# Channel weights folded into the transposes of the products, values by key straight from the projection, and a larger share of channel 14 for VectorE

## The chip, the cores and the metric

The kernel runs on one core of a Trainium2 chip. The metric is the device time of one execution in microseconds (us), lower is better. The core has TensorE (PE; its weight loads are listed as PEld), VectorE (DVE), ScalarE (ACT), GpSimd (POOL) and a queue of DMA issues (SP). Each engine runs its own instructions in the order in which they are written, and they wait for one another by semaphores.

## The reference, cut to what matters

Batch 8, sequence 512, width 128, 16 heads of 8 dimensions, 16 channels. Everything is float32.

```
Q, K, V = proj(Wq, bq), proj(Wk, bk), proj(Wv, bv)       # per head
for wl in 16 channels:
    m = cos(phase_modulators)[wl, head]
    scores = einsum('bhqd,bhkd->bhqk', Q*m, K*m) * SCALE  # = m*m * (Q.K) * SCALE
    scores = scores * cos(KERR * scores * scores)
    attn = softmax(scores)
    acc += einsum('bhqk,bhkd->bhqd', attn, V) * interference_weights[wl]
combined = (acc / 16) @ Wo + bo
```

After that come a residual sum, normalisation, a shared feed-forward block and 8 gated experts on 256 of the rows. The cosine factor is 1 in float32 for small scores; the kernel bounds the scores on the chip and takes a fast way (the one that runs here) in which it is left out.

## The kernel before

**Units.** The work is cut into 32 units: a unit is one head for four of the eight batch rows. Units 0 to 15 are group 0, units 16 to 31 group 1. For one unit the scores of keys against queries, 128 partitions x 8192 columns (4 key tiles x 4 batch rows x 512 queries), stand in `s_t`. They are the same for all 16 channels up to the factor m*m, so each channel is one exponential over them with another scale.

**ScalarE** takes the exponentials of channels 0 to 13 of a unit over all 8192 columns (L656), and of channel 14 over the first 7168 (`ACT_LAST`, L653). It writes one of two buffers `probs`, so exponential w+2 waits until TensorE has used that of w (`pv_done`).

**TensorE** multiplies each channel's exponentials with the values of the unit (L1273): per channel 16 products of a 27-column stationary operand with 512 moving columns, each of them two instructions, so 32 instructions. The stationary operand is `v_pad`: for each of 32 tiles of 128 keys, nine columns (8 value dimensions and a one for the denominators) in a field of zeros, so that three channels share a bank of PSUM (six banks' worth per unit, `W_GROUPS`; the fifth holds channels 12 to 14 and the sixth channel 15).

**VectorE** takes what is left of the exponentials in pieces of seven operations each (`piece_dve`, L720 to L743): four pieces of 2048 columns for channel 15, and a fifth piece of 1024 columns, the rest of channel 14. TensorE multiplies the pieces (`piece_pe`, L756). VectorE also copies each of the six groups of products to SBUF (`copy_products`, L1413), TensorE transposes it (`turn_products`, L1243, four transposes), and VectorE divides by the denominators, multiplies with the channel's weight and sums up (`weigh`, L1422 to L1443: reciprocal, times weight, times products, sum).

**Preparation of the next unit** is spread over the steps w = 0 to 14 of a unit (`prep_pe`, `prep_dve`): step 1 projects q, k and v (L785, three times four products of 32 stationary columns with 512 moving ones, the four in different columns of the array) and adds the biases (L859 to L861); steps 2 to 5 take scores and their maxima; step 6 transposes v (L808) and the maxima (L815) and copies v into `v_pad` (L869); steps 8 to 11 take the scores again and copy them to `s_t` (L877).

**The order** is written by hand. In step w TensorE does: the product of a piece that is due (`PRODUCT_STEPS`), the products of channel w, the transposes that are due (`TURN_STEPS`), the preparation. VectorE does in step w: the operations of pieces that are due (`PIECE_STEPS`), a copy (`COPY_STEPS`), a division (`TURN_STEPS`), the preparation. Some are due after the unit's end, in steps 0 to 2 of the next: the transposes of copy 4 (which is channel 15 and is made after the last piece in step 14) in step 0, and the product of the fifth piece in step 1, before the products of channel 1. In group 1 a pair of units also carries one chunk of the feed-forward block (`FF_STEPS`): TensorE, VectorE and GpSimd take turns in it.

## Time and profile before

| | |
|---|---|
| three runs | 3448.43, 3453.41, 3458.12 us (median 3453.41) |
| profiled execution | 3451.96 us, span 3449.9 us |
| ACT busy | 3334.6 us, 97% |
| DVE busy | 3152.2 us, 91% |
| PE busy / PEld busy | 2711.8 us, 79% / 778.2 us, 23% |
| mean granted TensorE clock | 0.909 of full speed |

Busy shares are of the span. PE's busy time holds modelled ends of matmuls. Adjacent instructions of an engine overlap a little at their ends, so the distance between two starts is somewhat less than the duration. The granted clock of TensorE has two levels here, 1.00 (2.4 GHz) and 0.50 (1.2 GHz).

### The profile page before, as it was taken

What the parts mean: (1) busy time and instruction counts of PE and PEld (TensorE: products, weight loads), DVE (VectorE), ACT (ScalarE), POOL (GpSimd) and SP (SyncE); (2) the same over time, 40 slices, a digit from 0 to 9 for tenths busy, and PEclk for the clock granted to TensorE, in tenths of its full rate; (3) what the DMA queues carried; (4) which work ended last, traced back from release to release, by engine and by line L of the source; (5) the groups of instructions that cost most, each with busy time, mean ns of one, the idle gap of its engine ahead of it and who ended that gap; (6) DMA issues with size and microseconds to landing.
All of it is one profiled execution on the core that took longest, in us unless ns stands there. A gap on an engine that the chain in (4) does not pass through costs nothing.

```text
span 3449.9 us, 47792 instructions
## 1 busy us (share of the span) xinstructions
PE 2711.8 (79%) x20599; PEld 778.2 (23%) x20599; DVE 3152.2 (91%) x2977; ACT 3334.6 (97%) x610; POOL 199.5 (6%) x325
## 2 busy tenths in 40 slices
PE   7887778887778887778887788887888887888763
PEld 2222222222222222222222222222222222222222
DVE  8899899899899899899899999999999999999977
ACT  7999999999999999999999999999999999999971
POOL 0000000000000000000010011110011110011111
PEclk8899999999999999999999999999999899999886
DMA  1000000000000000000000000000000000000010
GB/s 50 1 1 1 1 1 1 1 1 1 1 1 1 1 1 1 1 14 1 1 3 1 4 2 4 2 4 1 2 4 2 4 2 1 4 2 4 2 30 28
DMA packets 20759, 16.10 MB, mean 5 GB/s; under 512 B 4225, under 2 KB 18962, under 8 KB 20306
## 3 DMA queue, kind: packets, MB, share of 16 engines
q1 hardware_dynamic: 19282, 12.34, 1.2%
q8 instruction: 165, 2.70, 0.3%
q10 hardware_dynamic: 1152, 0.53, 0.1%
q0 software_dynamic: 128, 0.26, 0.0%
q14 instruction: 32, 0.26, 0.0%
HBM read 7.76 MB, written 5.37 MB: 4 GB/s over the span
## 4 chain that ended last, share of the span: by engine, by line
ACT 61%; issue 30%; ACTq 4%; DVE 3%; PE 2%; DMA 0%; SPq 0%; POOL 0%; DVEq 0%; POOLq 0%
ACT probs L656 56%; ACT probs L653 4%; ACTq L646 4%; PE psum L1273 1%; DVE m_pad L865 0%; ACTq L650 0%; DVE s_t L877 0%; ACT probs L680 0%; DVE probs L1190 0%; DVE probs L928 0%; DMA iw<-nterference_weights_dram 0%; SPq L468 0%; DVE x_p L743 0%; DVE x_p L735 0%; DVE x_p L739 0%
## 5 line engine op out<-in xcount | busy, mean ns | idle before, releaser
L656 ACT ACTIVATE probs<-s_t 128x8192 f32<-128x8192 f32 x447 | 3101.2, 7090 | 2.2 <-PE psum L1273 2.2
L1273 PE MATMUL psum<-probs,v_pad 128*27 128x512 f32 x15232 | 1992.5, 665 | 602.5 <-ACT probs L656 583.8
L1273 PEld LDWEIGHTS psum<-probs,v_pad 128*27 128x27 f32 x15232 | 485.3, 115 | 2036.1 <-issue 1095.5
L723 DVE SCALAR_TENSOR_TENSOR x_y<-s_t,c_last,x_2k 128x2048 f32<-128x2048 f32 (+1 forms) x160 | 344.1, 2150 | 2.3
L735 DVE SCALAR_TENSOR_TENSOR x_p<-x_p,x_y 128x2048 f32<-128x2048 f32 (+1 forms) x160 | 332.6, 2079 | 4.5
L743 DVE SCALAR_TENSOR_TENSOR x_p<-x_p,x_2k 128x2048 f32<-128x2048 f32 (+1 forms) x160 | 332.1, 2075 | 3.9
L731 DVE SCALAR_TENSOR_TENSOR x_p<-x_y 128x2048 f32<-128x2048 f32 (+1 forms) x160 | 330.9, 2068 | 3.3 <-PE psum L756 3.3
L739 DVE SCALAR_TENSOR_TENSOR x_p<-x_p 128x2048 f32<-128x2048 f32 (+1 forms) x160 | 331.5, 2072 | 2.4
L877 DVE COPY s_t<-psum 128x2048 f32<-128x2048 f32 x128 | 292.2, 2284 | 21.8 <-PE psum L839 21.1
L865 DVE TENSOR_REDUCE m_pad<-psum 128x4 f32<-128x2048 f32 x128 | 292.4, 2286 | 10.8 <-PE psum L802 9.7
L756 PE MATMUL psum<-x_p,v_pad 128*27 128x512 f32 x1152 | 174.5, 620 | 51.9 <-DVE x_p L743 51.4
L653 ACT ACTIVATE probs<-s_t,ln_one 128x7168 f32<-128x7168 f32 x32 | 202.5, 6327 | 0.0
L720 DVE TENSOR_SCALAR x_2k<-s_t,c_last 128x2048 int16<-128x2048 f32 (+1 forms) x160 | 188.2, 1176 | 4.4 <-issue 1.0
L1422 DVE RECIPROCAL r_z<-psum 128x48 f32<-128x48 f32 (+1 forms) x192 | 80.2, 418 | 108.5 <-PE psum L1243 108.4
L1413 DVE COPY o_sb<-psum 128x512 f32<-128x512 f32 x192 | 131.4, 684 | 28.4 <-PE psum L1273 27.1
L802 PE MATMUL psum<-k_t,q_t 8*128 8x512 f32 x1024 | 147.7, 647 | 2.7 <-DVE m_pad L865 2.4
L839 PE MATMUL psum<-q_t,k_t 9*128 9x512 f32 x1024 | 147.6, 647 | 1.6 <-DVE s_t L877 1.5
L1243 PE MATMUL psum<-ident,o_sb 128*128 128x128 f32 x768 | 125.9, 286 | 1.0 <-DVE weighted L1429 1.0
L494 POOL COPY w_head<-w_qkv 128x24 f32 x32 | 27.7, 866 | 1659.6 <-ACT probs L656 1639.8
L1243 PEld LDWEIGHTS psum<-ident,o_sb 128*128 128x128 f32 x768 | 80.5, 141 | 166.0 <-issue 164.8
L727 DVE TENSOR_SCALAR x_2k<-x_2k 128x2048 int16<-128x2048 int16 (+1 forms) x160 | 105.0, 656 | 5.5
L505 POOL TENSOR_TENSOR loop_memory<-loop_memory 128x2 f32<-128x2 f32 x24 | 27.0, 1123 | 1415.8 <-DVE loop_memory L928 1415.8
(240 smaller groups left out, 1116.0 us busy)
## 6 DMA issues: line engine op xcount, KB each, us to landing
s_t<-in_L_attn_x_dram SPq DMA_DIRECT2D x4, 256.0 KB, 6.9
x_next_dram<-x_p SPq DMA_DIRECT2D x1, 1024.0 KB, 4.5
x_group<-x_next_dram SPq DMA_DIRECT2D x1, 1024.0 KB, 4.9
loop_memory<-in_L_attn_x_dram SPq DMA_DIRECT2D x8, 128.0 KB, 2.2
x_dram<-loop_memory SPq DMA_DIRECT2D x8, 128.0 KB, 1.8
out_dram<-loop_memory SPq DMA_DIRECT2D x8, 128.0 KB, 1.8
x_dram<-probs SPq DMA_DIRECT2D x2, 512.0 KB, 3.3
out_dram<-probs SPq DMA_DIRECT2D x2, 512.0 KB, 3.6
```

The costliest lines, as they stand in the source:

```text
L653: nc.scalar.activation(probs[:, (p + w) % 2, 0:ACT_LAST], s_t[:, p, 0:ACT_LAST], ACT.Exp, bias=ln_one[:, 0:1], scale=scales[(p + w) % 2]). ...
L656: nc.scalar.activation(probs[:, (p + w) % 2, :], s_t[:, p, :], ACT.Exp, scale=scales[(p + w) % 2]).then_inc(s["exp_done"], 1)
L720: nc.vector.tensor_scalar(at, scores, scale, LOWEST_Y, ALU.mult, ALU.max).then_inc(s["piece_chain"], 1)
L723: nc.vector.scalar_tensor_tensor(out=y, in0=scores, scalar=scale, in1=at, op0=ALU.mult, op1=ALU.subtract) \
L731: nc.vector.scalar_tensor_tensor(out=t, in0=y, scalar=EXP2_A, in1=y, op0=ALU.add, op1=ALU.mult) \
L735: nc.vector.scalar_tensor_tensor(out=t, in0=t, scalar=EXP2_B, in1=y, op0=ALU.add, op1=ALU.mult) \
L739: nc.vector.scalar_tensor_tensor(out=t, in0=t, scalar=EXP2_C, in1=t, op0=ALU.add, op1=ALU.mult) \
L743: nc.vector.scalar_tensor_tensor(out=t, in0=t, scalar=EXP2_D, in1=x_2k[:, 0:cols], op0=ALU.add, op1=ALU.mult) \
L865: nc.vector.tensor_reduce(m_pad[:, qt, :].rearrange("p (b l) -> p b l", l=L)[:, :, R_M:R_M + 1], banks(qt), AX.X, ALU.max, negate=True).th ...
L877: nc.vector.tensor_copy(s_t[:, p, kt * NB * S:(kt + 1) * NB * S], banks(kt).rearrange("p b q -> p (b q)")).then_inc(s["st_copied"], 1)
L1243: last = nc.tensor.transpose(psum[:, 6, qt * P:(qt + 1) * P], o_sb[:, at % 2, qt * P:(qt + 1) * P], ident[:])
L1273: last = nc.tensor.matmul(products_of(u, wg)[L * b:L * b + SLOTS * A, :], v_pad[:, p, b * T + kt, c0:c0 + SLOTS * A], probs[:, (p + w) % 2 ...
```

## The change

Three things are changed. (1) The products are no longer transposed against the identity and weighted afterwards: `turn_products` is now a matmul with a diagonal matrix (`turn_w`, one per group of channels, made once by `turn_weights_dve` in some 14 short operations before the first unit). Its diagonal has the channel's weight on the value rows and 1 on the denominators' rows, and the extra multiplication in `weigh` goes. (2) The values come by key straight from TensorE: 16 matmuls with 128 columns of `x_group` stationary and nine moving columns of the head's weights replace the third projection, the transposes of v and the copy into `v_pad`; the bias is added on the way into `v_pad`. (3) `SHARED_B` becomes (0, 1): VectorE's fifth piece has 2048 columns in group 0 and 1536 in group 1 instead of 1024, and ScalarE's exponential of channel 14 has 6144 and 6656 columns instead of 7168.

```diff
@@ -40,8 +40,8 @@
 X_COLS = NB * S
-SHARED_B = 2
-ACT_LAST = T * X_COLS - (NB - SHARED_B) * S
+SHARED_B = (0, 1)
+ACT_LAST = [T * X_COLS - (NB - b) * S for b in SHARED_B]
 PIECES = T + 1
@@ -135,6 +135,8 @@
         ident = sb("ident", [P, P])
+        turn_w = sb("turn_w", [P, NWG, P])
+        v_bias = sb("v_bias", [P, H, A])
         w_qkv = sb("w_qkv", [P, 3, E])
@@ -650,7 +652,7 @@
                         if w == WA - 1:
-                            nc.scalar.activation(probs[:, (p + w) % 2, 0:ACT_LAST], s_t[:, p, 0:ACT_LAST], ACT.Exp,
+                            nc.scalar.activation(probs[:, (p + w) % 2, 0:ACT_LAST[g]], s_t[:, p, 0:ACT_LAST[g]], ACT.Exp,
                                                  bias=ln_one[:, 0:1], scale=scales[(p + w) % 2]).then_inc(s["exp_done"], 1)
@@ -711,7 +713,7 @@
             piece, base = u * PIECES + n, (u * PIECES + n) * PIECE_LINKS
-            w, start, cols = (W - 1, n * X_COLS, X_COLS) if n < T else (WA - 1, ACT_LAST, T * X_COLS - ACT_LAST)
+            w, start, cols = (W - 1, n * X_COLS, X_COLS) if n < T else (WA - 1, ACT_LAST[u // H], T * X_COLS - ACT_LAST[u // H])
             scores = s_t[:, p, start:start + cols]
@@ -751,8 +753,8 @@
             c0 = VPAD if n < T else VPAD - A * SLOT_OF[WA - 1]
-            for b in range(NB) if n < T else range(SHARED_B, NB):
-                at = b * S if n < T else (b - SHARED_B) * S
+            for b in range(NB) if n < T else range(SHARED_B[u // H], NB):
+                at = b * S if n < T else (b - SHARED_B[u // H]) * S
                 last = nc.tensor.matmul(products_of(u, wg)[L * b:L * b + SLOTS * A, :],
@@ -778,14 +780,17 @@
                     pe.wait_ge(s["xg_loaded"], group * 16 + 16)
-                for i in range(3):
+                for i in range(2):
                     for b in range(NB):
...
                             pe.wait_ge(s["x_copied"], b + 1)
-                        last = nc.tensor.matmul(psum[L * b:L * b + L, 5 if first and i == 2 else i, :], w_head[:, p, i, :],
+                        last = nc.tensor.matmul(prep[L * b:L * b + L, i, :], w_head[:, p, i, :],
                                                 x_group[:, b * S:(b + 1) * S], start=True, stop=True)
-                    if first and i == 1:
-                        last.then_inc(s["qk_projected"], 1)
+                if first:
+                    last.then_inc(s["qk_projected"], 1)
+                for j in range(GT):
+                    last = nc.tensor.matmul(psum[:, 5 if first else 2, j * A:(j + 1) * A], x_group[:, j * P:(j + 1) * P],
+                                            w_head[:, p, 2, 0:A], start=True, stop=True)
                 last.then_inc(s["proj_done"], 1)
@@ -804,8 +809,6 @@
                 pe.wait_ge(s["max_done"], n * T + T - int(first))
-                for qt in range(T):
-                    nc.tensor.transpose(prep[:, 1, qt * P:(qt + 1) * P], v_t[:, qt * P:(qt + 1) * P], ident[:])
                 if first:
@@ -851,12 +881,13 @@
                 dve.wait_ge(s["proj_done"], 1)
-                nc.vector.tensor_scalar(v_t[:], psum[:, 5, :], b_head[:, p, 2:3], None, ALU.add)
+                dve.wait_ge(s["v_biased"], 1)
+                values_dve(n, p, psum[:, 5, :])
                 dve.wait_ge(s["w_summed"], 1)
...
                 dve.wait_ge(s["proj_done"], n + 1)
-                nc.vector.tensor_scalar(v_t[:], prep[:, 2, :], b_head[:, p, 2:3], None, ALU.add)
+                values_dve(n, p, prep[:, 2, :])
                 nc.vector.tensor_scalar(q_t[:], prep[:, 0, :], b_head[:, p, 0:1], SCALE, ALU.add, ALU.mult)
@@ -866,8 +897,6 @@
                 dve.wait_ge(s["mrow_done"], n + 1)
-                nc.vector.tensor_copy(v_pad[:, p, :, VPAD:VPAD + A].rearrange("p (b t) e -> p t b e", b=NB),
-                                      prep[:, 1, :].rearrange("p (t b l) -> p t b l", t=T, b=NB)[:, :, :, 0:A])
                 dve.wait_ge(s["qkv_ready"], n + 1)
@@ -1237,11 +1266,13 @@
                     n1 = v * NWG + (at + 1)
+                    if n1 == 1:
+                        pe.wait_ge(s["turn_ready"], 1)
                     pe.wait_ge(s["o_copied"], n1 + 2)
...
                     for qt in range(T):
-                        last = nc.tensor.transpose(psum[:, 6, qt * P:(qt + 1) * P],
-                                                   o_sb[:, at % 2, qt * P:(qt + 1) * P], ident[:])
+                        last = nc.tensor.matmul(psum[:, 6, qt * P:(qt + 1) * P], o_sb[:, at % 2, qt * P:(qt + 1) * P],
+                                                turn_w[:, GROUP_AT[at], :], start=True, stop=True)
                     last.then_inc(s["ot_done"], 1)
@@ -1268,13 +1299,13 @@
                         for kt in range(T):
-                            for b in range(SHARED_B if w == WA - 1 and kt == T - 1 else NB):
+                            for b in range(SHARED_B[g] if w == WA - 1 and kt == T - 1 else NB):
                                 at = (kt * NB + b) * S
...
                                     start=(kt == 0 and w in FIRST_OF),
-                                    stop=(w in LAST_OF and kt == (T - 2 if u == UNITS - 1 and w == WA - 1 and b >= SHARED_B else T - 1)))
+                                    stop=(w in LAST_OF and kt == (T - 2 if u == UNITS - 1 and w == WA - 1 and b >= SHARED_B[g] else T - 1)))
                         last.then_inc(s["pv_done"], 1)
@@ -1320,6 +1351,7 @@
             nc.vector.memset(v_pad[:], 0.0)
+            nc.vector.memset(v_bias[:, :, D:A], 1.0)
             nc.vector.memset(r_z[:], 0.0).then_inc(s["pv_done"], 3)
@@ -1354,6 +1386,7 @@
             by_dim = row_dim.rearrange("p (i o d) -> p i o d", i=1, o=1).broadcast_to([P, 3, H, D])
+            nc.vector.tensor_copy(v_bias[:, :, 0:D], b_rows[:, 2, :].rearrange("p (h d) -> p h d", d=D)).then_inc(s["v_biased"], 1)
             link(nc.vector.tensor_tensor(b_own.rearrange("p i (h d) -> p i h d", d=D),
@@ -1400,6 +1433,8 @@
             with dve.If(fast == 1):
+                turn_weights_dve(dve)
+
                 def copy_products(v, at):
@@ -1420,10 +1455,7 @@
                     nc.vector.reciprocal(rz, ot[:, :, :, D]).then_inc(s["rz_done"], 1)
-                    dve.wait_ge(s["rz_done"], n1 * 2 - 1)
-                    nc.vector.tensor_tensor(rz, rz, iw[:, w0:w0 + n].rearrange("p (o r) -> p o r", o=1)
-                                            .broadcast_to([P, GT, n]), ALU.mult).then_inc(s["rz_done"], 1)
-                    dve.wait_ge(s["rz_done"], n1 * 2)
+                    dve.wait_ge(s["rz_done"], n1)
                     dst = (weighted if at else summed)[:, 0:n, :]
```

## Rows read from the trace of the kernel before

**Rows 1.** Waits of ACT, 40 to 3338 us: total, times, longest.

```profile
ACT probs L656 <- PE psum L1273: 2.2, 2, 1.2
```

**Rows 2.** Timeline of ACT over one unit: start, length, line, count.

```profile
235.06 6.29 ACT L653 ACTIVATE probs<-s_t,ln_one 128x7168 f32<-128x7168 f32 x1
241.24 97.05 ACT L656 ACTIVATE probs<-s_t 128x8192 f32<-128x8192 f32 x14
```

**Rows 3.** Groups of ACT by form: count, busy us, mean ns.

```profile
L633 ACT ACTIVATE probs<-s_t 128x2048 f32<-128x2048 f32 x4 | 7.6, 1910 | 3.7 <-DVE s_t L877 3.7
```

**Rows 4.** Windows: us, PE, PEld, DVE, ACT, POOL busy, clock, DMA (units 2-15, 16-30).

```profile
241.40:1686.60 1445.20, 1149.25 (x8868) 315.06 (x8872) 1319.41 (x1111) 1445.20 (x211) 8.17 (x28) 0.93 0.01 2
1686.60:3235.00 1548.40, 1256.20 (x9589) 352.46 (x9585) 1458.03 (x1352) 1546.17 (x233) 155.80 (x242) 0.92 0.01 3
```

**Rows 5.** Groups of DVE by form: count, busy us, mean ns.

```profile
L731 DVE SCALAR_TENSOR_TENSOR x_p<-x_y 128x2048 f32<-128x2048 f32 x128 | 292.1, 2282 | 3.3 <-PE psum L756 3.3
L720 DVE TENSOR_SCALAR x_2k<-s_t,c_last 128x2048 int16<-128x2048 f32 x128 | 164.1, 1282 | 3.3 <-issue 1.0
...
L727 DVE TENSOR_SCALAR x_2k<-x_2k 128x2048 int16<-128x2048 int16 x128 | 91.4, 714 | 4.4
...
L731 DVE SCALAR_TENSOR_TENSOR x_p<-x_y 128x1024 f32<-128x1024 f32 x32 | 38.8, 1212 | 0.0
L1424 DVE TENSOR_TENSOR r_z<-r_z,iw 128x48 f32<-128x48 f32 x160 | 33.3, 208 | 5.5
L720 DVE TENSOR_SCALAR x_2k<-s_t,c_last 128x1024 int16<-128x1024 f32 x32 | 24.1, 753 | 1.1
L859 DVE TENSOR_SCALAR v_t<-psum,b_head 128x512 f32<-128x512 f32 x31 | 23.1, 746 | 26.1 <-PE psum L785 26.1
...
L727 DVE TENSOR_SCALAR x_2k<-x_2k 128x1024 int16<-128x1024 int16 x32 | 13.7, 427 | 1.1
L869 DVE COPY v_pad<-psum 128x144 f32<-128x144 f32 x32 | 9.7, 302 | 0.6 <-PE psum L815 0.6
```

**Rows 6.** Timeline of DVE, end of unit 7 and start of unit 8.

```profile
837.23 0.46 DVE L1422 RECIPROCAL r_z<-psum 128x48 f32<-128x48 f32 x1 [2.93 <-PE psum L1243]
...
865.48 0.68 DVE L1413 COPY o_sb<-psum 128x512 f32<-128x512 f32 x1
```

**Rows 7.** Timeline of ACT: channel 0 of unit 8.

```profile
859.71 7.06 ACT L656 ACTIVATE probs<-s_t 128x8192 f32<-128x8192 f32 x1
```

**Rows 8.** Timeline of PE, start of unit 7 (ACT begins it at 756.64).

```profile
763.73 5.20 PE L1273 MATMUL psum<-probs,v_pad 128*27 128x512 f32 x32 [3.30 <-ACT probs L656]
768.86 0.66 PE L1243 MATMUL psum<-ident,o_sb 128*128 128x128 f32 x4
...
770.64 3.64 PE L1273 MATMUL psum<-probs,v_pad 128*27 128x512 f32 x32 [0.15 <-ACT probs L656]
774.10 2.76 PE L785 MATMUL psum<-x_group,w_head 128*32 128x512 f32 x24
777.57 3.64 PE L1273 MATMUL psum<-probs,v_pad 128*27 128x512 f32 x32 [0.72 <-ACT probs L656]
```

**Rows 9.** Windows again: 32 loads for 128 moving columns; four for nine.

```profile
3350.10:3354.20 4.10, 4.07 (x33) 3.87 (x32) 1.27 (x2) 0.60 (x1) 2.67 (x1) 0.91 0.15 40
...
3383.50:3384.30 0.80, 0.78 (x4) 0.78 (x4) 0.80 (x1) 0.00 (x0) 0.00 (x0) 0.50 0.00 0
```

**Rows 10.** Timeline of DVE, start of unit 29.

```profile
3035.26 0.68 DVE L1413 COPY o_sb<-psum 128x512 f32<-128x512 f32 x1
...
3043.28 0.42 DVE L981 COPY loop_memory<-psum 128x256 f32<-128x256 f32 x1
```

**Rows 11.** Timeline of ACT: channel 0 of unit 29.

```profile
3026.93 7.02 ACT L656 ACTIVATE probs<-s_t 128x8192 f32<-128x8192 f32 x1
```

**Rows 12.** Timeline of PE in unit 29, products of channel 2.

```profile
3047.86 3.64 PE L1273 MATMUL psum<-probs,v_pad 128*27 128x512 f32 x32
```

**Rows 13.** Timeline of PE, the first projection.

```profile
11.26 4.23 PE L785 MATMUL psum<-x_group,w_head 128*32 128x512 f32 x24
```

25 lines of the change are left out of this document (24 added, 1 removed).

## The prediction

> **What bounds the kernel now.** I read the waits of ScalarE first: between 40 and 3338 us the only wait on TensorE in its exponentials is 2.2 us in all [rows 1], and in the windows over units 2 to 15 it is busy for the whole 1445.2 us [rows 4]. So ScalarE sets the pace. Its timeline gives the unit: fourteen exponentials of 8192 columns take 97.05 us, a start every 6.92 or 6.93 us, and that of channel 14 has 6.18 us from its start to the next [rows 2]: 103.1 us a unit, 32 times. The other engines matter only where they hand something to ScalarE late. VectorE is the fuller of them: idle (1445.2 - 1319.4) / 14 = 9.0 us a unit in group 0 and (1548.4 - 1458.0) / 15 = 6.0 us in group 1; TensorE is idle (1445.2 - 1149.3) / 14 = 21 us [rows 4]. What decides below is not these sums but TensorE's order around a unit's first three channels.
>
> **What ScalarE saves.** One exponential has 7.06 us for 8192 columns and 1.91 us for 2048 [rows 3, 7], so (7.06 - 1.91) / 6144 = 0.84 ns a column: 0.86 us for 1024 columns fewer in each of 16 units, 0.43 us for 512 fewer in the 16 others, together 20.6 us. The lower bound is the pitch that the present cut bought, 6.93 - 6.18 = 0.75 us for 1024 columns [rows 2]: 18 us. I take the first.
>
> **What VectorE gets.** The fifth piece has seven operations. Five are of the form of the first row (2282 against 1212 ns for 2048 and 1024 columns), one goes from 753 to 1282, one from 427 to 714 [rows 5]: 5 x 1.07 + 0.53 + 0.29 = 6.2 us in group 0, half of it, 3.1 us, in group 1. Removed are six multiplications of 0.21 us, the copy into v_pad of 0.30, and of the 0.75 us for v's bias some 0.44, if an addition over 144 columns costs what the copy over 144 does [rows 5]: 2.0 us. Net +4.2 and +1.1 us, against 9.0 and 6.0 us idle and a unit shorter by 0.86 and 0.43: it still fits on average, with about 4 us left in both groups.
>
> **What TensorE gets.** The third projection was a third of 24 instructions in 2.76 us, 0.92 us [rows 8]. Its place is taken by 16 matmuls of two instructions, each with its own load of 128 columns. Thirty-two such loads with 128 moving columns took 3.87 us at a granted clock of 0.91, 0.121 us each; four loads for nine moving columns took 0.78 us at a clock of 0.50, 0.195 each, which would be 0.098 at full clock [rows 9]. The two hardly differ once brought to one clock, so the load sets the price: 3.1 to 3.9 us, I take 3.4, or 2.5 more than now. The weighted transposes are now eight instructions at the same price, 0.9 us instead of 0.66 [rows 8], six times a unit; the transposes of v go (0.6). Together +3.5 us a unit against 21 us idle: nothing on average.
>
> The Trainium skill (TensorE: Matmul & The Clock Gate, on LDWEIGHTS) prices a load by its columns, 128 / 1.2 = 107 ns, which would be 3.4 us here; the same page's table of back-to-back cycles gives about 60 cycles (25 ns) for 1 to 64 moving columns, which would make the 32 matmuls 0.8 us. By the second the projection would be no dearer than now; that is the rival below. The four loads of [rows 9] speak for the first.
>
> **Where it meets: group 0.** Count from the start of a unit's channel 0 on ScalarE. Now VectorE leaves the wait for the third group's transposes at 837.23 and is then busy without a gap until the copy of channel 15's products starts at 865.48 and ends some 0.6 us later, 6.4 us after ScalarE's 859.71 [rows 6, 7]. With the change this copy comes later by 6.2 (the piece), less 0.4 (two multiplications in that stretch), plus 0.3 (the transposes it waited for are longer), plus 0.86 (ScalarE begins the unit earlier). I add 0.8, an estimate between 0 and 1.1, for the third piece's product, which stands in TensorE's queue ahead of channel 10's: VectorE leaves step 1 later than now, with little idle time to catch up in before step 10. Sum: 14.1 us.
>
> TensorE's queue has, in this order: products of channel 0, the transposes of that copy, the product of the fifth piece, products of channel 1, the projections, products of channel 2. Now channel 0's products end 12.2 us into the unit and the transposes find their copy ready; those of channel 2 end at 777.57 + 3.64 - 756.64 = 24.6 us [rows 8]. ScalarE needs them for channel 4, at 4 x 6.92 = 27.7 us, so 3.1 us are in hand. With the change TensorE stands before the transposes until 14.1, and then come 0.9, 1.0 (a full piece), 3.5 (channel 1, 774.10 - 770.64), 1.85 (two thirds of 2.76), 3.4 and 3.6: 28.35 us, with handovers about 28.5. ScalarE waits 0.8 us in every unit. At full clock, the 0.86 us saved are given back.
>
> Then the clock. Channel 0's products took 5.20 us after an idle stretch of 3.30 us, where the same 32 instructions take 3.64 elsewhere [rows 8]: part of them ran at the lower of the two levels, for 1.6 us. The new wait leaves TensorE idle for 2 to 3.5 us just ahead of a chain with no slack, so a part of that chain will run at 1.2 GHz: between 0 and 1.6 us more, I take 1.0. The Trainium skill's page on TensorE (section Why this matters for your kernels) advises against idle gaps of this kind between bursts, since the clock then falls back; it speaks against this change, and would put the whole 1.6 here, 10 us more in the sum. With 1.0: 16 x (0.8 + 1.0 - 0.86) = +15 us.
>
> **Group 1.** A 1536-column piece moves the copy by 3.1 - 0.4 + 0.3 + 0.43 = 3.4 us. In odd units a link of the feed-forward block is in the way: TensorE's four small matmuls between channel 1's products and the projections wait for VectorE's copy that ends at 3043.28 + 0.42 - 3026.93 = 16.8 us [rows 10, 11], and channel 2's products end at 24.6 [rows 12], again 3.1 in hand. That copy moves to about 20.0 (one more multiplication gone). Then 0.6, 1.85, 3.4, 3.6 give 29.4: late by 1.7 us in seven units, 12 us. In even units the copy at about 12.3 leads to 26.3 us, 1.4 in hand; 2 us for all of them for the clock. Less 6.9 saved: +7 us.
>
> **Start and end.** The first projections ran 24 instructions in 4.23 us [rows 13]; the third of them, 1.4, becomes 32 loads at 0.195, 6.2 us, since the clock is low there: +5 us, as the first scores stand behind it in the queue and nothing covers it. The diagonal matrices, some 14 short operations of 0.2 us, come when VectorE enters the first unit, where it runs ahead of TensorE: nothing. The end has two longer transposes and two multiplications fewer: nothing.
>
> **Sum.** 3451.96 + 15 + 7 + 5 = 3479 us. The profiled execution is 1.5 us below the median of the runs shown, which I leave in the rounding. A difference under 0.3% (10 us) can't be told from none here, so "same" is 3443 to 3464.
>
> **Rivals.**
> - *Cheap nine-column matmuls* (other side). If the 32 instructions take no more than 2.6 us, 0.08 each, channel 2's products end before 27.7 at full clock and ScalarE never waits; the bound is the ScalarE saving alone. 3452 - 20.6 + 2 to 5 for the start = 3433 to 3436 us. For it: the products have an idle 21 us a unit to hide in, and no row shows nine columns at the full clock. Against it: [rows 9]. Chance 0.28, with the case that I place the copy 1 to 2 us too late.
> - *Late, but at full clock*. The stall is 0.8 us in group 0 and 1.0 or so in odd units of group 1: 3452 - 13.7 + 12.8 - 6.9 + 7 + 5 = 3456 us. For it: the chain is dense, and once TensorE works it recovers. Chance 0.22.
> - *VectorE becomes the bound.* It would need more than the 4 us left; 103.1 - 9.0 + 4.2 = 98.3 against 102.2. It would take an addition or a wait that I don't see; the time would be some 3465 us. Inside the slower case, 0.03.
> - *The cut on ScalarE buys less than it says*, 0.75 us for 1024 columns: 18 us instead of 20.6. It moves every case by 2.6.
>
> **Chances.** Forecast (late, and partly at the low clock) 0.50, own range 3464 to 3500; full clock 0.22; cheap matmuls 0.28. Faster 0.28, same 0.22, slower 0.50. The range 3434 to 3500 takes in the rival's time and the stall with all of 1.6 us for the clock.
>
> **What would show it.** In the changed profile: waits of ScalarE on the products of the channels' line, near 1.8 us once a unit, before channel 4; TensorE idle before the transposes of channel 15's copy, released by that copy; the v projection at 3.1 to 3.9 us for 32 instructions; the fifth piece at 13.5 and 10.4 us. Wrong it is if ScalarE still has no wait (then 3433 to 3436), if the 32 instructions take under 2.6 us, or if the copy ends before 13 us into the unit.

## The result and the profile after

| | before (same chip) | changed kernel |
|---|---|---|
| median of four runs | 3450.92 us | 3535.27 us |
| lowest to highest | 3447.97 to 3458.12 | 3534.28 to 3538.72 |
| profiled execution, span | 3451.96, 3449.9 | 3535.03, 3533.0 |
| mean granted TensorE clock | 0.909 | 0.901 |

The ratio is 1.0243 (95% interval 1.0224 to 1.0262): slower by 84 us. The forecast was slower by 27, and its range ended at 3500. So the sign was right and the size was not.

The first row to read is again the waits of ScalarE between 40 us and the end of the last unit (total, times, longest). It answers to [rows 1].

```profile
ACT probs L658 <- PE psum L1304: 93.6, 60, 5.2
```

From 2.2 us in two waits it has gone to 93.6 us in sixty. Against this stand the 20.8 us that ScalarE saves, and the start: the first unit's exponentials run 5.1 us later than before (its second begins at 47.15 us instead of 42.02). 93.6 - 2.2 - 20.8 + 5.1 = 76 of the 83 us by which the span grew. Another 6 us are lost at the waits themselves: an exponential that starts behind a wait doesn't overlap the one before it (7.0 us long, against 6.93 from start to start), and so the mean distance of two starts, waits taken off, is 6.941 us instead of 6.927. The first exponential of channel 14 begins at 139.41 us instead of 131.99; of these 7.4 us, 5.1 are the start and 2.15 the first unit's wait before channel 4. The unit, from one exponential of channel 14 to the next, has gone from 103.08 to 105.62 us in group 0 and from 103.36 to 105.63 in group 1, where ScalarE alone would need 102.2 and 102.6.

The timeline of ACT over one unit of group 0 answers to [rows 2] (start, length, line, count; in brackets the idle time before and what ended it):

```profile
348.08 5.40 ACT L655 ACTIVATE probs<-s_t,ln_one 128x6144 f32<-128x6144 f32 x1
353.39 27.78 ACT L658 ACTIVATE probs<-s_t 128x8192 f32<-128x8192 f32 x4
383.45 34.72 ACT L658 ACTIVATE probs<-s_t 128x8192 f32<-128x8192 f32 x5 [2.27 <-PE psum L1304]
419.15 34.73 ACT L658 ACTIVATE probs<-s_t 128x8192 f32<-128x8192 f32 x5 [0.98 <-PE psum L1304]
453.79 5.40 ACT L655 ACTIVATE probs<-s_t,ln_one 128x6144 f32<-128x6144 f32 x1
```

There are two waits in the unit: 2.27 us before channel 4, which was forecast (it is 1.7 to 2.5 us in most units, 0.6 in four and 5.2 in three), and 0.98 us before channel 9, which was not. Over the thirty-one units the waits before channel 4 come to 70.0 us (38.4 and 31.6 in the two groups) and those before channel 9 to 22.9 (10.8 and 12.1); 0.7 stand before channel 3.

TensorE in the same unit, which shows both chains (it answers to [rows 8]):

```profile
360.47 6.15 PE L1304 MATMUL psum<-probs,v_pad 128*27 128x512 f32 x32 [3.94 <-ACT probs L658]
367.15 1.16 PE L1274 MATMUL psum<-turn_w,o_sb 128*128 128x128 f32 x8 [0.53 <-DVE o_sb L1448]
368.24 1.06 PE L758 MATMUL psum<-x_p,v_pad 128*27 128x512 f32 x8
369.12 3.62 PE L1304 MATMUL psum<-probs,v_pad 128*27 128x512 f32 x32
372.55 1.90 PE L787 MATMUL psum<-x_group,w_head 128*32 128x512 f32 x16
374.38 3.74 PE L792 MATMUL psum<-w_head,x_group 128*128 128x9 f32 x32
378.05 5.33 PE L1304 MATMUL psum<-probs,v_pad 128*27 128x512 f32 x32
...
412.89 1.52 PE L758 MATMUL psum<-x_p,v_pad 128*27 128x512 f32 x8 [3.86 <-DVE x_p L745]
414.17 4.92 PE L1304 MATMUL psum<-probs,v_pad 128*27 128x512 f32 x32
```

Channel 0's exponentials are multiplied, TensorE stands before the transposes until VectorE's copy is there, and from 367.15 it works without a gap to 383.38; ScalarE starts channel 4 at 383.45. The second chain is at the end: TensorE stands 3.86 us for the last operation of piece 1 (the second piece of channel 15), and channel 7's products behind it end at 419.09; channel 9 starts at 419.15. They took 4.92 us there, where the same 32 instructions take 3.62 at full clock.

The next unit has the same order in both places, and these stretches run at full clock. ScalarE waits only 0.56 us before channel 4 and not at all before channel 9:

```profile
480.07 3.74 PE L792 MATMUL psum<-w_head,x_group 128*128 128x9 f32 x32
483.74 3.64 PE L1304 MATMUL psum<-probs,v_pad 128*27 128x512 f32 x32
...
516.89 1.06 PE L758 MATMUL psum<-x_p,v_pad 128*27 128x512 f32 x8 [2.60 <-DVE x_p L745]
517.77 3.62 PE L1304 MATMUL psum<-probs,v_pad 128*27 128x512 f32 x32
```

VectorE's side of both (answering to [rows 6]):

```profile
366.41 0.68 DVE L1448 COPY o_sb<-psum 128x512 f32<-128x512 f32 x1
...
410.55 2.29 DVE L745 SCALAR_TENSOR_TENSOR x_p<-x_p,x_2k 128x2048 f32<-128x2048 f32 x1
```

The groups by form, answering to [rows 5]: an operation of the pieces in its two sizes, and the values' addition (count, busy us, mean ns; idle before and what ended it).

```profile
L733 DVE SCALAR_TENSOR_TENSOR x_p<-x_y 128x2048 f32<-128x2048 f32 x144 | 328.8, 2283 | 3.2 <-PE psum L758 3.2
L733 DVE SCALAR_TENSOR_TENSOR x_p<-x_y 128x1536 f32<-128x1536 f32 x16 | 27.9, 1742 | 0.0
L870 DVE TENSOR_TENSOR v_pad<-psum,v_bias 128x144 f32<-128x144 f32 x32 | 9.8, 306 | 35.6 <-PE psum L792 35.6
```

Windows over the two groups, answering to [rows 4] (us, PE, PEld, DVE, ACT, POOL busy, clock, DMA):

```profile
139.40:1724.00 1584.60, 1317.50 (x10144) 436.94 (x10148) 1475.01 (x1081) 1536.91 (x227) 21.17 (x30) 0.91 0.01 2
1724.00:3414.00 1690.00, 1427.05 (x10840) 476.56 (x10832) 1578.26 (x1337) 1646.28 (x248) 205.40 (x263) 0.91 0.01 3
```

No engine is full any more. In group 0 ScalarE is idle 3%, VectorE 7% and TensorE 17% of the time. This is a pipeline that waits in turn, not one that is bound by an engine.

### The profile page after: what moved, and what is told of

It reads as the page before. It is cut to its first block, busy times and chain, and to the rows that moved or that the text cites. A ratio compares the mean times of both kernels' runs of the same rounds, so it can differ in the third digit from the quotient of the medians.

```text
span 3533.0 us, 50435 instructions
## 1 busy us (share of the span) xinstructions
PE 2902.6 (82%) x22007; PEld 993.0 (28%) x22007; DVE 3245.3 (92%) x2769; ACT 3320.4 (94%) x610; POOL 244.7 (7%) x325
## 4 chain that ended last, share of the span: by engine, by line
issue 38%; DVE 29%; PE 18%; ACT 9%; POOL 5%; DMA 0%; ACTq 0%; POOLq 0%; SPq 0%; DVEq 0%
PE psum L1304 11%; ACT probs L658 8%; DVE x_p L745 4%; DVE m_pad L896 4%; DVE x_p L741 3%; DVE x_y L725 3%; DVE x_p L737 3%; DVE x_p L733 3%; DVE s_t L906 3%; PE psum L792 2%; PE psum L758 2%; PE psum L1274 2%; DVE x_2k L722 1%; PE psum L787 1%; DVE r_z L1457 1%
## 5 line engine op out<-in xcount | busy, mean ns | idle before, releaser
L658 ACT ACTIVATE probs<-s_t 128x8192 f32<-128x8192 f32 x447 | 3104.1, 7021 | 93.6 <-PE psum L1304 93.6
L725 DVE SCALAR_TENSOR_TENSOR x_y<-s_t,c_last,x_2k 128x2048 f32<-128x2048 f32 (+1 forms) x160 | 370.1, 2313 | 2.3
L737 DVE SCALAR_TENSOR_TENSOR x_p<-x_p,x_y 128x2048 f32<-128x2048 f32 (+1 forms) x160 | 358.3, 2239 | 4.5
L745 DVE SCALAR_TENSOR_TENSOR x_p<-x_p,x_2k 128x2048 f32<-128x2048 f32 (+1 forms) x160 | 357.7, 2236 | 3.9
L741 DVE SCALAR_TENSOR_TENSOR x_p<-x_p 128x2048 f32<-128x2048 f32 (+1 forms) x160 | 357.4, 2233 | 2.4
L733 DVE SCALAR_TENSOR_TENSOR x_p<-x_y 128x2048 f32<-128x2048 f32 (+1 forms) x160 | 356.6, 2229 | 3.2 <-PE psum L758 3.2
L758 PE MATMUL psum<-x_p,v_pad 128*27 128x512 f32 x1248 | 191.0, 674 | 112.5 <-DVE x_p L745 112.0
L1274 PE MATMUL psum<-turn_w,o_sb 128*128 128x128 f32 x1536 | 222.5, 288 | 24.9 <-DVE o_sb L1448 24.2
L1274 PEld LDWEIGHTS psum<-turn_w,o_sb 128*128 128x128 f32 x1536 | 185.9, 191 | 190.0 <-issue 143.7
L655 ACT ACTIVATE probs<-s_t,ln_one 128x6144 f32<-128x6144 f32 (+1 forms) x32 | 179.8, 5619 | 0.0
L792 PEld LDWEIGHTS psum<-w_head,x_group 128*128 128x128 f32 x1024 | 121.2, 198 | 26.8 <-issue 26.8
```

What stands on the lines that cost most here:

```text
L658: nc.scalar.activation(probs[:, (p + w) % 2, :], s_t[:, p, :], ACT.Exp, scale=scales[(p + w) % 2]).then_inc(s["exp_done"], 1)
L725: nc.vector.scalar_tensor_tensor(out=y, in0=scores, scalar=scale, in1=at, op0=ALU.mult, op1=ALU.subtract) \
L733: nc.vector.scalar_tensor_tensor(out=t, in0=y, scalar=EXP2_A, in1=y, op0=ALU.add, op1=ALU.mult) \
L737: nc.vector.scalar_tensor_tensor(out=t, in0=t, scalar=EXP2_B, in1=y, op0=ALU.add, op1=ALU.mult) \
L741: nc.vector.scalar_tensor_tensor(out=t, in0=t, scalar=EXP2_C, in1=t, op0=ALU.add, op1=ALU.mult) \
L745: nc.vector.scalar_tensor_tensor(out=t, in0=t, scalar=EXP2_D, in1=x_2k[:, 0:cols], op0=ALU.add, op1=ALU.mult) \
```

## The experiments

Three parts make up the change: (1) the channel weights in the transposes, (2) the values straight from TensorE, (3) the larger fifth piece. All kernels are the changed one with the edit shown; "undone" means the code of before. Each was timed beside the kernel before on the same chip (3449.6 to 3451.2 us).

**Parts undone, one or two at a time.** e1 leaves only part 3.

```diff
-  matmul(psum.., o_sb.., turn_w[:, GROUP_AT[at], :])      # part 1 undone
+  transpose(psum.., o_sb.., ident), and r_z * iw on VectorE
-  for j in range(GT): matmul(.., x_group[..], w_head[:, p, 2, 0:A])   # part 2 undone
+  third projection as for q and k, transposes of v_t, copy to v_pad
```

> Part 3 of the change alone (VectorE's fifth piece 2048 and 1536 columns), on the kernel before; its projections, its transposes and its multiplications. Theory A (ScalarE waits because TensorE's chain from the copy of channel 15's products to the products of channel 2 ends after 27.7 us of the unit; here without the 32 loads it is 14 + 0.7 + 1.0 + 3.5 + 2.8 + 3.6 = 25.6 us): no wait of ScalarE in group 0 at full clock, at most part of the saving of 20 us lost to the clock: 3430 to 3450 us. Theory B (VectorE is too full: its work without waits is 103.1 - 9.0 + 6.2 = 100.3 us a unit plus waits that it can't avoid): as slow as with the whole change or slower, 3500 to 3550 us.

Measured: 3507.6 us, ratio 1.0161 (1.0137 to 1.0185). The wait before channel 4 is gone, as the prediction's chain says. But the kernel is 58 us slower than before and not 20 faster, and the waits (75.6 us) stand before channel 9 (21.7 us in group 0, 43.1 in group 1) and channel 3 (9.4). ACT's timeline of one unit shows one of each:

```profile
349.62 20.88 ACT L658 ACTIVATE probs<-s_t 128x8192 f32<-128x8192 f32 x3
371.24 41.65 ACT L658 ACTIVATE probs<-s_t 128x8192 f32<-128x8192 f32 x6 [0.74 <-PE psum L1302]
414.61 34.73 ACT L658 ACTIVATE probs<-s_t 128x8192 f32<-128x8192 f32 x5 [1.72 <-PE psum L1302]
```

The larger piece, which was priced against 9.0 and 6.0 us of idle time on VectorE, is not free even without the loads.

e2 undoes part 1 alone:

> The changed kernel without part 1: the products are transposed against the identity and multiplied by the weights afterwards, as before. Theory A: the chain is shorter by one weighted transposition (0.5 us), still late: ScalarE's waits 0.5 to 1 us a unit shorter than the 2.3 before channel 4, 3505 to 3525 us. Theory B (VectorE too full): VectorE has 1.5 us a unit more, so slower than with the whole change, 3550 to 3580 us. Theory C (the weighted transposes as such cost, six times a unit 0.5 us on TensorE): 3480 us or less.

Measured: 3567.0 us, 1.0334 (1.0305 to 1.0363), 32 us slower than the full change. Waits 121.6 us: 80 before channel 4, 31 before channel 9, 10 before channel 3. The six multiplications that part 1 takes from VectorE are needed beside the larger piece.

e3 undoes part 2 alone:

> The changed kernel without part 2: v is projected with q and k, transposed and copied as before. Theory A: TensorE's chain ends at 14.1 + 1.1 + 1.0 + 3.5 + 2.8 + 3.6 = 26.1 us, before the 27.7 at which ScalarE needs it: no wait before channel 4, no 5 us more at the start, 3432 to 3455 us. Theory B (VectorE too full): it has 0.7 us a unit more to do, 3535 to 3560 us.

Measured: 3491.89 us, 1.0114 (1.009 to 1.0138). 43 us of the 84 go with the loads, and with them every wait before channel 4. Left are 62.0 us, 50 of it before channel 9, where the whole change has 22.9: a wait that goes at one place can come back at the next, so the waits of two kernels can't be subtracted place by place.

```profile
513.33 34.72 ACT L658 ACTIVATE probs<-s_t 128x8192 f32<-128x8192 f32 x5 [0.77 <-PE psum L1304]
```

e4 undoes part 3 alone:

```diff
-SHARED_B = (0, 1)
+SHARED_B = (2, 2)
```

> The changed kernel without part 3: the fifth piece has 1024 columns in all units, ScalarE's exponential of channel 14 has 7168 as before. Theory A: VectorE's copy comes 7 us earlier, the 32 loads alone make channel 2's products end at about 26.5 us of the unit in group 0, before 27.7; odd units of group 1 have no margin left (16.8 + 0.6 + 1.9 + 3.7 + 3.6 = 26.6). No saving and 7 us more at the start: 3457 to 3480 us. Theory B: VectorE has more room than before the change: 3457 us and no waits of ScalarE. Theory D (the 32 loads alone do it, whatever the piece): above 3500 us.

Measured: 3507.08 us, 1.0156 (1.0132 to 1.0181). Without any larger piece the loads alone still cost, before channels 4 and 9 alike (28 and 25 us).

e10 and e16 complete the table, with part 1 alone and part 2 alone:

> Part 1 alone on the kernel before: weighted transposes, 1.5 us a unit less for VectorE, 3 us a unit more for TensorE in six places of 0.5 us. Theory G: no piece is later than before, nothing comes late: 3445 to 3456 us. Theory C (the weighted transposes as such cost): 3470 us or more.

Measured: 3451.88 us, 1.0005 (0.9995 to 1.0014). The longer transposes (1.16 us instead of 0.66, six times a unit) cost nothing, and by themselves bring nothing.

> Part 2 alone on the kernel before. Theory A: the chain in step 0 to 2 is 12.2 + 0.7 + 0.6 + 3.5 + 1.9 + 3.7 + 3.6 = 26.2 us where channel 0's products ran at the low clock, 1.5 in hand; but channel 7's products have only 1.7 us in hand in the kernel before, and VectorE leaves step 1 some 3 us later: waits before channel 4 and 9 as in the kernel with parts 1 and 2 (24 and 36 us), 3500 to 3520 us. If part 2 needs part 1 to cost: 3455 to 3465 us.

Measured: 3499.55 us, 1.0145 (1.013 to 1.0159); 40.6 us of waits.

Difference of the medians against before on the same chip, in us:

| part | 1 | 2 | 3 | 1+2 | 1+3 | 2+3 | 1+2+3 |
|---|---|---|---|---|---|---|---|
| time | +1 | +50 | +58 | +58 | +42 | +117 | +84 |

Parts 2 and 3 each cost 50 to 60 us alone, although part 3 alone saves ScalarE 20. Part 1 gives 16 us back beside part 3 and 33 beside both, and nothing beside part 2 alone (+58 against +50, which the intervals don't tell apart).

**The second chain.** Piece 1's product stands in step 7 ahead of channel 7's products. e6 moves it one step on:

```diff
-PRODUCT_STEPS = {5: 0, 7: 1, 10: 2, 14: 3, WA + 1: 4}
+PRODUCT_STEPS = {5: 0, 8: 1, 10: 2, 14: 3, WA + 1: 4}
```

> The whole change, with the second piece's product in TensorE's step 8 instead of step 7, so that the products of channel 7 no longer stand behind a piece that VectorE has not finished. Theory G (the wait before channel 9 is TensorE standing in front of that piece): the wait before channel 9, 0.65 us a unit in group 0 and 0.9 in group 1, goes, the one before channel 4 stays: 3505 to 3520 us. If both waits are one loop that VectorE sets, the time only moves to channel 4: 3525 to 3540 us.

Measured: 3503.95 us, 1.0167 (1.0134 to 1.0199), 31 us faster than the change. No wait before channel 9 is left; those before channel 4 stay (56 us of the 61.8 in all). The edit takes away two things at once: TensorE no longer stands for the piece ahead of channel 7's products, and in the unit shown these are back at full clock, 3.64 us.

```profile
351.23 27.80 ACT L658 ACTIVATE probs<-s_t 128x8192 f32<-128x8192 f32 x4
381.28 69.33 ACT L658 ACTIVATE probs<-s_t 128x8192 f32<-128x8192 f32 x10 [2.25 <-PE psum L1304]
```

**The clock.** e5 gives TensorE 16 more instructions at the end of steps 14, 0 and 6, so that it does not stand idle before the chains (in units 1 to 30):

```diff
+  if w in (14, 0) or (w == 6, after the preparation):
+      16 instructions of matmul(prep[.., 1, :], ident[:, 0:L], turn_w[.., 0:S])
```

> The whole change, and in units 1 to 30 sixteen more instructions of TensorE (a product of the identity with constants, written to a bank that is free, 1.9 us at full clock) in three places where it stood idle: after the products of channel 14, before the weighted transposes in step 0, and before the product of the second piece in step 7. They compute nothing that is used. Theory E (the idle stretches bring the clock to 1.2 GHz and the chains behind them then come late; that is most of ScalarE's 2.3 us before channel 4 and all of the 1 us before channel 9): with the stretches filled the low clock moves away from the chains, 3460 to 3500 us. Theory F (the chains are late at any clock): no gain, or slower by what the filler delays, 3530 to 3560 us.

Measured: 3517.33 us, 1.0182 (1.0161 to 1.0202), clock 0.922 instead of 0.901. TensorE in one unit:

```profile
363.70 3.64 PE L1304 MATMUL psum<-probs,v_pad 128*27 128x512 f32 x32 [2.22 <-ACT probs L658]
...
377.62 3.74 PE L792 MATMUL psum<-w_head,x_group 128*128 128x9 f32 x32
381.29 5.33 PE L1304 MATMUL psum<-probs,v_pad 128*27 128x512 f32 x32
```

Channel 0's products, ahead of the chain, are back at 3.64 us from 6.15. Those of channel 2, in the chain, stay at 5.33. The idle time ahead of the chain is not what slows it. The time came out between the theories. In the profiled run, the slowest of the four (3530.96 us), the waits before channel 9 have halved, to 11 us, those before channel 4 are still 68, and 10 us stand before channel 3.

**The loads in another place.** e7 issues the 32 loads in step 12 instead of step 1 and adds the bias in step 13; e8 does this and moves piece 1's product.

```diff
+  if step == 12 and not first: the GT matmuls of w_head[:, p, 2, 0:A]
+  channel 0's products of the next unit wait for values_ready, which VectorE's addition sets
```

> The whole change, with the 32 loads of the values' projection moved from step 1 to step 12 of TensorE, where it is idle for 2 to 3 us, and the addition of the bias to VectorE's step 13. Theory A (the chain from the copy to channel 2's products): it loses 3.7 us, so no wait before channel 4; what is left is the wait before channel 9, at most 1.7 us a unit as in the kernel without part 2: 3460 to 3495 us. If the loads only push the stall to the end of the unit: 3520 us or more.

> The values' projection in step 12 and the second piece's product in step 8, with the whole change otherwise. If the two waits (before channel 4 and before channel 9) are all that stands between the change and its saving: 3430 to 3445 us, faster than before the change. If VectorE is the limit behind them, 3470 us or more.

Measured: e7 3519.58 us, 1.02 (1.0181 to 1.0218); e8 3496.54 us, 1.0138 (1.0115 to 1.0162). The wait before channel 4 is gone and stands before channel 0 instead (30.5 and 33.1 us in the two groups of e7). TensorE and ACT in e7, at the end of a unit:

```profile
444.17 4.56 PE L833 MATMUL psum<-w_head,x_group 128*128 128x9 f32 x32
448.66 6.11 PE L1316 MATMUL psum<-probs,v_pad 128*27 128x512 f32 x32
...
454.85 20.89 ACT L658 ACTIVATE probs<-s_t 128x8192 f32<-128x8192 f32 x3 [3.77 <-PE psum L1316]
```

The loads now stand ahead of channel 13's products, whose buffer channel 0 of the next unit needs. These took 6.11 us behind the loads and ended at 454.77. All 30 waits before channel 0 in e7 and all 28 in e8 end in this way; the new wait for `values_ready` never held TensorE up. ACT in e8:

```profile
353.30 97.03 ACT L658 ACTIVATE probs<-s_t 128x8192 f32<-128x8192 f32 x14 [3.77 <-PE psum L1316]
```

e11 and e12 put them in the middle: all in step 6, or half each in steps 6 and 7, both with piece 1's product in step 8.

```diff
+  if step == 6 and not first: the GT matmuls            # e11
+  if step in (6, 7) and not first: GT // 2 of them      # e12
+  VectorE adds the bias in step 7 (e11) or 8 (e12), and TensorE's step 8 waits for it
```

> The whole change with the second piece's product in step 8 and the values' projection in step 6, after the transposes of the maxima, where TensorE stood idle for 2 and 4 us. Theory G: the 32 loads end at about 56.5 us of the unit, channel 7's products at about 60, before the 62.3 at which ScalarE needs them; nothing before channels 0 to 4 is touched: 3432 to 3455 us. Theory H: 3480 us or more, with waits elsewhere.

> As with the values' projection in step 6, but half of the loads in step 6 and half in step 7. At full clock no difference from the undivided one; at 1.2 GHz the undivided loads take some 7 us and are late, the halves are not: if the low clock matters there, this one is faster by 5 to 20 us, 3430 to 3450 us.

Measured: 3554.77 us, 1.0307 (1.0282 to 1.0333) and 3552.11 us, 1.0287 (1.0267 to 1.0307), worse than the change by some 18 us; halving the loads made no difference clear of noise. Waits 109 us in 80 places each. TensorE in e11:

```profile
401.69 5.54 PE L832 MATMUL psum<-w_head,x_group 128*128 128x9 f32 x32
407.16 4.98 PE L1317 MATMUL psum<-probs,v_pad 128*27 128x512 f32 x32
```

Here the loads themselves took 5.54 us, and channel 7's products behind them 4.98. The move also brings a new wait: before the scores of step 8 TensorE stands for VectorE's addition, 20.4 us in all in e11 and 113.0 in e12. So the two kernels don't price the loads' place alone. TensorE is idle for a sixth of the time, and yet there is no place among four tried where these 3.7 us cost nothing.

**Two loads in sixteen.** e15 leaves the order of the changed kernel and takes most of the loads away; it leaves out the values of the other fourteen tiles, so what it computes is not the result.

```diff
-  for j in range(GT):
+  for j in range(GT) if first else range(2):
```

> The whole change, but from the second unit on only two of the 16 matmuls of the values' projection (4 loads instead of 32); VectorE and ScalarE do all that they do with the change. The values of the other 14 tiles are left out. Theory A (the loads on TensorE are what part 2 costs): the wait before channel 4 goes, 3485 to 3495 us, as in the kernel without part 2 or a few us less, since VectorE has less to do here. If it is VectorE's place in step 1 that costs, 3510 us or more.

Measured: 3482.55 us, 1.0089 (1.0075 to 1.0104): the other fourteen matmuls cost 53 us of the 84. Group 0 is back at 102.58 us a unit; in group 1 the waits before channel 9 stay (21.7 us). TensorE in one unit:

```profile
367.57 1.90 PE L787 MATMUL psum<-x_group,w_head 128*32 128x512 f32 x16
369.40 0.61 PE L792 MATMUL psum<-w_head,x_group 128*128 128x9 f32 x4
369.94 3.64 PE L1304 MATMUL psum<-probs,v_pad 128*27 128x512 f32 x32
```

Here is what the earlier runs had left open. Behind four instructions with their own loads channel 2's products take 3.64 us, behind 32 they took 5.33, with no idle time between in either. Over all units:

| kernel | channel 2's products over 4 us | their mean |
|---|---|---|
| before | 0 of 29 units | 3.65 us |
| changed | 27 of 31 | 5.21 |
| e5, filler | 21 of 30 | 4.88 |
| e6 | 16 of 30 | 4.61 |
| e16, part 2 alone | 17 of 31 | 4.64 |
| e4, parts 1 and 2 | 16 of 29 | 4.74 |
| e3, without part 2 | 0 of 27 | 3.66 |
| e15, four of 32 | 0 of 30 | 3.64 |

(Unit 31, which prepares nothing, and units whose 32 instructions the trace splits are left out.) The windows show it in one unit of the changed kernel (columns as in [rows 4]): the loads, then the two halves of the products behind them.

```profile
374.40:378.00 3.60, 3.60 (x36) 3.60 (x32) 2.92 (x3) 3.60 (x1) 0.00 (x0) 1.00 0.00 0
378.10:380.70 2.60, 2.60 (x21) 0.77 (x24) 2.54 (x4) 2.60 (x1) 0.00 (x0) 0.72 0.00 0
380.70:383.30 2.60, 2.60 (x16) 0.42 (x8) 1.28 (x1) 0.47 (x1) 0.00 (x0) 0.63 0.00 0
```

The granted clock is 1.00 during the loads and 0.72 and 0.63 behind them, although TensorE is busy throughout. In units 0 to 30 it was never seen without the 32 loads, but they are not enough: units 1, 4, 8 and 12 of the changed kernel have the same order, and there channel 2's products take 3.64 us. Nor are they the only way to it: in unit 31, with no projection ahead, these products took 5.25 us in the kernel before. e15 also shortens the stretch by 3.1 us, and no run separates that from the loads.

**Towards a version that gains.** e9 undoes part 2 and moves piece 1's product to step 8, with the full part 3:

> The changed kernel without part 2 (v as before) and with the second piece's product in step 8. Theory G (two separate places: before channel 4 the 32 loads, before channel 9 the product of a piece that VectorE has not finished): both are gone; of ScalarE's waits in the kernel without part 2 (28 and 43 us in the groups) those before channel 9 (25 and 35) go: 3430 to 3450 us. Theory H (VectorE is late in general, and the wait turns up at the next place in TensorE's order that needs a piece or a copy): 3465 to 3490 us.

Measured: 3467.75 us, 1.0059 (1.0036 to 1.0082). The eight units from the first channel 14 on run at ScalarE's need, 102.21 us each:

```profile
137.67 97.00 ACT L658 ACTIVATE probs<-s_t 128x8192 f32<-128x8192 f32 x14
234.57 5.40 ACT L655 ACTIVATE probs<-s_t,ln_one 128x6144 f32<-128x6144 f32 x1
239.88 96.99 ACT L658 ACTIVATE probs<-s_t 128x8192 f32<-128x8192 f32 x14
```

Group 0's mean is 102.66 us, group 1's 104.89, where the feed-forward work also stands on VectorE. So the cut is taken back where it does not fit:

```diff
+  part 2 undone, piece 1's product in step 8
-SHARED_B = (0, 1)
+SHARED_B = (0, 2)      # e13;  (1, 2) in e14
```

> Weighted transposes, v as before, the second piece's product in step 8, and the cut of group 0 only: a fifth piece of 2048 columns in units 0 to 15, of 1024 as before in units 16 to 31. If the waits of group 1 with 1536 columns (33 us in the kernel with both cuts) come from its fuller VectorE: group 0 at 102.2 to 102.7 us a unit, group 1 at 103.4 as before, 3438 to 3447 us. If they come from the moved product: 3455 us or more.

> The same with 1536 columns in group 0 and 1024 in group 1. ScalarE then needs 102.65 us a unit in group 0: 3443 to 3448 us, and if the margins are what matters, no wait of ScalarE in group 0.

Measured: e13 3449.04 us, 0.9996 (0.9982 to 1.0011), no change. e14 3442.93 us, 0.9977 (0.9967 to 0.9986): 7 us faster than before, the one version that beats both kernels. It has the weights in the transposes, piece 1's product in step 8, and 1536 columns for VectorE in group 0 only. The waits are 3.9 us in four places, and group 0's unit is 102.70 us (the window shown begins with channel 1):

```profile
349.52 90.08 ACT L658 ACTIVATE probs<-s_t 128x8192 f32<-128x8192 f32 x13
439.51 5.83 ACT L655 ACTIVATE probs<-s_t,ln_one 128x6656 f32<-128x6656 f32 x1
```

## Why the prediction was right in its sign and wrong in its size

**Right: the first chain at full clock.** In group 0 the copy of channel 15's products ends 366.41 + 0.68 - 353.39 = 13.7 us into the unit (forecast 14.1; my limit of 13 was not reached), TensorE stands before the transposes until it comes, the 32 instructions take 3.74 us (forecast 3.1 to 3.9, I took 3.4), and channel 2's products begin at 24.7 us. In the units where they run at full clock they end at 28.3 (forecast 28.35) and ScalarE waits 0.6 us (forecast 0.8). The weighted transposes took 1.16 us each where I took 0.9. e1 and e3, which have no such loads, have no such wait. The rival of cheap nine-column matmuls is out: 0.117 us each, where it needed 0.08. So is the one at full clock.

**Failed: the clock term.** I put 1.0 us a unit for the low clock in group 0 and 2 us for all of group 1, 18 us together, and gave as its cause the new idle time ahead of the chain. Channel 2's products took 5.3 us instead of 3.64 in 24 units, and 6.2 to 6.3 in three. At full clock a unit of group 0 is 0.6 us late, an odd unit of group 1 0.8 and an even one 0.1 (the start of channel 2's products, and 3.64). So 16 of the 70 us before channel 4 are lateness at full clock, where the forecast's terms had 16 x 0.8 + 12 = 25, and 54 are the clock. This is the largest error of the sum. The cause was wrong too, for the most part. e5 removed the slow products ahead of the chain and left those within it; e15 kept the idle time ahead (3.94 us, and channel 0's products at 6.48) and they were gone; and in odd units of group 1 TensorE does not stand before the transposes at all, and they are there. They come behind the 32 loads. Only in the three units with 5.2 us is the forecast's cause there as well: TensorE stands 3.05 us before the transposes, and channel 1's products behind them take 4.95 us instead of 3.62. That the sum had a clock term in this place, and with it a time clear of "same", was largely luck. Part 2's price on TensorE is then (3.74 - 0.92) + 1.56 = 4.4 us a unit, against 2.5 and 1.0 in the forecast. The change on TensorE alone, 4.4 us and 0.5 for the longer transposes, is more than the 3.1 us that this chain had in hand [rows 8]. In e16, with the smaller piece and the short transposes, 23 of the 50 us are waits before channel 4; another 18 stand before channel 9, and VectorE itself waits longer for the projection (103.7 us in all at L870, where the kernel before has 26.1 at L859). Rows of either kernel's loads at full clock, such as [rows 9], could not show what follows them.

The Trainium skill (TensorE: Matmul & The Clock Gate, on LDWEIGHTS) prices a load of 128 columns at 107 ns; the 3.74 us for 32 agree, at 117. The same page's advice against idle gaps before bursts was cited for the whole 1.6 us. The trace agrees with it for channel 0's products (6.15 us behind 3.94 us idle, 3.64 with the filler), but these are not in the chain.

**Failed: "it still fits on average".** This is the step of the piece on VectorE, priced at +6.2 and +3.1 us a unit against 9.0 and 6.0 idle. I looked for one place where the lateness meets TensorE and allowed 0.8 us for another. But VectorE's lateness is carried into the next handover, and the order in TensorE's queue turns it into lateness of the products. The place was step 7, where before TensorE had this order:

```profile
805.27 6.61 PE L1273 MATMUL psum<-probs,v_pad 128*27 128x512 f32 x32 [2.22 <-ACT probs L656]
...
812.83 1.06 PE L756 MATMUL psum<-x_p,v_pad 128*27 128x512 f32 x8
813.71 3.62 PE L1273 MATMUL psum<-probs,v_pad 128*27 128x512 f32 x32
```

and VectorE's last operation for that product:

```profile
809.11 2.29 DVE L743 SCALAR_TENSOR_TENSOR x_p<-x_p,x_2k 128x2048 f32<-128x2048 f32 x1
```

It ended at 811.40, and channel 7's products at 817.33, 1.7 us before ScalarE needed them for channel 9 (756.64 + 9 x 6.93 = 819.0); in most units of group 0 it is 2.8 us. That is less than the 3.1 us in which the prediction looked for the bound. In the changed kernel VectorE ends the operation 410.55 + 2.29 - 353.39 = 59.5 us into the unit, where it was 54.8, and TensorE's queue waits 3.86 us for it.

Lateness alone did not make the wait. In units 1, 4, 8 and 12 channel 7's products run at full clock and end 0.7 us before channel 9 needs them. In all 26 units with a wait they took 4.1 to 4.9 us instead of 3.62, and with the piece's product (up to 1.5 us instead of 1.06) the low clock added 1.4 to 1.8 us to waits of 0.6 to 1.3. It was so before as well: the 2.2 us of [rows 1] stand in the two units where these products took 4.88 and 4.72 us. So the larger piece took most of what was in hand and the clock the rest. e6 takes both away: the 23 us of waits before channel 9 go, and 31 us of time. That TensorE's standing for the piece is what lowers the clock there is likely, and was not tried alone. In e1, which has this chain and not the first, 65 us of waits before channel 9 and 9 before channel 3 take the place of the 20 us saved; in its group 1, 13 of the 43 us before channel 9 are more than the clock added.

**Failed: group 1.** Forecast: odd units 1.7 us late, even units in hand, and the smaller piece cheap. Measured: both kinds wait, 2.1 us a unit before channel 4 and 0.8 before channel 9. An even unit had 1.4 us in hand by the forecast's own sum, and none at full clock: its copy ended 13.2 us into the unit (12.3 forecast), and the loads and the transposes took 0.6 more than I took. The clock behind the loads then makes the 1.7 us that it waits. An odd unit is 0.8 us late at full clock and waits 2.4. The rival at full clock had 7 us for the odd units where the same sum gives 12; at 12 it would have said 3461.

**The start** was as forecast, 5.1 us for 5, but not in its parts: the 32 loads took 4.93 us (I took 6.2), and the other two projections 3.61, where two thirds of the 4.23 of [rows 13] are 2.8:

```profile
11.58 3.61 PE L787 MATMUL psum<-x_group,w_head 128*32 128x512 f32 x16 [0.18 <-DVE x_group L1385]
15.11 4.93 PE L792 MATMUL psum<-w_head,x_group 128*128 128x9 f32 x32
```

**ScalarE's saving** was as forecast, to the column: 6.18 us from the start of channel 14 to the next before, 5.31 now [rows 2], 0.87 for 1024 columns.

**The sum.** Forecast: +15 for group 0, +7 for group 1, +5 for the start. Measured: 15 x (105.62 - 103.08) = 38 and 16 x (105.63 - 103.36) = 36 us for the two groups, 7.4 and 0.5 for start and end. That is 82 us where the terms of the forecast gave 27. Of the 55 us between, 27 are the waits before channel 4 (70 us, where the forecast's terms had 16 x 1.8 + 12 + 2 = 43: 9 less of lateness and 36 more of the clock), 21 the waits before channels 9 and 3 less those of the kernel before, and 6 the overlap lost at the waits.

**Open.** Why the clock falls behind loads only in some units (16 to 27 of 30) was not settled; unit times in the changed kernel recur in patterns (105.7, 105.7, 102.9, 105.7, 109.0 in group 0), as do the units in which channel 2's products are slow, but no run separates which follows from which. Nor was the order of e11 and e12 tried without their new wait for the values.

## What to carry to other kernels

Judge work put on an engine with idle time by the smallest time in hand at any handover behind it in that engine's order and in the queues that wait for it, all round the unit, not by the average idle time: here 9.0 us idle a unit hid nothing, because one handover had 1.7 us and another 3.1, and a stretch at the low clock takes 1.4 to 1.8 of them. Where many matmuls with few columns replace few with many, price each by its load, and look for the clock behind them. When several parts are changed together, time each alone: one of these three was free, and useful beside the larger piece, and it was hidden by the two others.

## What the hardware showed that was not expected

- A dense run of 32 loads with nine moving columns each ran at a granted clock of 1.00, and the clock fell in the 32 full-width instructions right behind it, which took 5.33 us instead of 3.64, without a gap between. In other places the loads were slow as well (4.56 us in e7, 5.54 in e11). With 4 such instructions instead of 32 it never did (0 of 30 units), nor with three full-width projections (0 of 29).
- Every wait of ScalarE before channel 9, in the kernel before, the changed one and e1 to e5, stood in a unit in which channel 7's products ran partly at the low clock (over 4.0 us instead of 3.62).
- A matmul of nine moving columns costs nearly as much as one of 128: 32 instructions in 3.74 us (0.117 each) against eight in 1.16 us (0.145) in the weighted transposes. The plain transposes of the same tiles are four instructions in 0.66 us.
- Filler on TensorE raised the mean granted clock from 0.901 to 0.922 and gave back 18 us; the products behind the loads stayed slow in 21 of 30 units.
